# Row units in halves of 512 keys through a ring of three banks, and a down accumulator in the fourth

## The reference

```python
xn = layernorm(x)
q, k, v = (bitnet_linear(xn, w, s) for w, s in ((wq, sq), (wk, sk), (wv, sv)))
scores = einsum('bhqd,bhkd->bhqk', q, repeat(k, 4)) / 4
out = einsum('bhqk,bhkd->bhqd', softmax(scores), repeat(v, 4))
attn = bitnet_linear(out, wo, so)
ffn = (silu(xn @ gate.T) * (xn @ up.T)) @ down.T
return x + attn + ffn
```

## Time and profile before

| what | value |
| --- | --- |
| three timed runs, median (lowest to highest) | 507.28 us (506.56 to 508.65) |
| profiled execution | 506.6 us |
| its span, first to last instruction | 504.9 us |
| granted clock of PE, mean of the span | 0.996 |
| DVE busy in the span | 417.0 us |
| ACT busy in the span | 351.2 us |

### The profile page before, as it was taken

How to read it: one execution, slowest core, us unless ns; L and a number is a source line. 1 busy time by engine, 2 the same in 40 slices (tenths; PEclk the granted TensorE clock), 3 DMA queues, 4 the chain that set the end, 5 groups by cost and what they waited for, 6 DMA issues and landing times.

```text
span 504.9 us, 10418 instructions
## 1 busy us (share of the span) xinstructions
PE 482.1 (95%) x4218; PEld 163.1 (32%) x4218; DVE 417.0 (83%) x487; ACT 351.2 (70%) x655; POOL 93.6 (19%) x138
## 2 busy tenths in 40 slices
PE   1899999999999999999999999999999999999996
PEld 1564444433332222222222222222222223333442
DVE  7879869676778999999999999999999962223985
ACT  1943643352338999999999999999999987874000
POOL 4212245434323000000000000000000103142021
PEclk9999999999998999999999999999999999999999
DMA  8853763732004602102111111120220104463321
GB/s 267 270 94 95 172 142 42 196 76 32 13 0 66 123 23 63 40 24 64 40 32 54 41 49 37 42 61 23 49 55 24 49 28 111 111 152 101 106 79 46
DMA packets 31302, 39.02 MB, mean 77 GB/s; under 512 B 6608, under 2 KB 20816, under 8 KB 31256
## 3 DMA queue, kind: packets, MB, share of 16 engines
q1 hardware_dynamic: 22232, 27.34, 18.8%
q0 software_dynamic: 8304, 10.95, 11.6%
q10 hardware_dynamic: 720, 0.08, 0.1%
HBM read 33.24 MB, written 10.35 MB: 86 GB/s over the span
## 4 chain that ended last, share of the span: by engine, by line
PE 79%; ACT 8%; DVE 6%; DMA 4%; issue 2%; SPq 0%; ACTq 0%; DVEq 0%
PE ps L1257 23%; PE ps L1109 19%; PE ps L1221 13%; PE ps L1118 9%; ACT room L688 6%; PE ps L1183 5%; PE ps L1088 3%; PE ps L1288 3%; DVE nmx L821 3%; PE ps L1170 2%; DMA rsum<-o_scratch 2%; ACT osb L699 1%; DMA hlo<-x 1%; DMA ga<-r_scratch 1%; DVE stats L747 1%
## 5 line engine op out<-in xcount | busy, mean ns | idle before, releaser
L821 DVE TENSOR_REDUCE nmx<-ps 128x1 f32<-128x1024 f32 x256 | 293.8, 1217 | 15.6 <-PE ps L1118 15.4
L688 ACT ACTIVATE room<-ps 128x512 f32<-128x512 f32 x512 | 272.6, 598 | 19.9 <-PE ps L1221 10.0
L1257 PE MATMUL ps<-room,vcur 128*32 128x256 f32 (+1 forms) x1912 | 160.5, 407 | 4.5 <-ACT osb L699 4.1
L1221 PE MATMUL ps<-qst,kB 50*128 50x512 f16 x512 | 148.2, 384 | 1.2 <-DVE room L920 0.5
L1118 PE MATMUL ps<-kA,qst 48*128 48x512 f16 x512 | 145.9, 384 | 0.0
L1109 PE MATMUL ps<-room,wf 128*128 128x512 f16 x448 | 100.6, 379 | 0.0
L1257 PEld LDWEIGHTS ps<-room,vcur 128*32 128x32 f32 x1912 | 37.7, 108 | 103.5 <-issue 56.9
L1221 PEld LDWEIGHTS ps<-qst,kB 50*128 50x128 f16 x512 | 29.8, 93 | 100.2 <-ACT room L688 88.1
L669 ACT ACTIVATE room<-ps,gsc 128x512 f32<-128x512 f32 x28 | 19.2, 686 | 61.0 <-PE ps L1109 61.0
L1109 PEld LDWEIGHTS ps<-room,wf 128*128 128x128 f16 x448 | 42.4, 98 | 55.1 <-issue 7.2
L527 POOL TENSOR_TENSOR hlo<-room,hhi 128x512 f16<-128x512 f32 x28 | 34.0, 1216 | 87.7 <-ACT hhi L599 87.7
(11 more groups left out here) (131 smaller groups left out, 290.5 us busy)
## 6 DMA issues: line engine op xcount, KB each, us to landing
qst<-q_scratch SPq DMA_DIRECT2D x32, 192.0 KB, 3.6
o_scratch<-osb SPq DMA_DIRECT2D x16, 256.0 KB, 2.2
q_scratch<-parts SPq DMA_DIRECT2D x12, 256.0 KB
hlo<-x SPq DMA_DIRECT2D x8, 256.0 KB, 4.9
parts<-x POOLq DMA_DIRECT2D x8, 256.0 KB, 3.4
wf<-gate POOLq DMA_DIRECT2D x14, 128.0 KB, 3.7
wf<-up POOLq DMA_DIRECT2D x14, 128.0 KB, 5.7
wd<-down POOLq DMA_DIRECT2D x1, 1792.0 KB, 13.7
```

The source lines that it names most:

```text
L688: nc.scalar.activation(probs[:, s % 2, r, :], ps[:, bank_of(gp, s, i), :], ACT.Exp, scale=gam_reg[par][r]).then_inc(scores_free, 1)
L821: nc.vector.tensor_reduce(nmx[:, hf, idx:idx + 1], bank_pair(idx % 2), AX.X, ALU.max, negate=True).then_inc(rows_free, 1)
L1221: nc.tensor.matmul(ps[:, bank_of(gp, s, i), :], kB[low:low + SROWS, par, kt % (TT // 2) * P:(kt % (TT // 2) + 1) * P], qst[low:low + SROWS ...
L1257: mm = nc.tensor.matmul(ps[32 * r:32 * r + 32, 7, of], vcur[:, par, key_tile(r, j), :], probs[:, s % 2, r, of], start=(j == 0 and part == ...
```

## The change

Row units of the loop are now computed and reduced tile by tile. Tile n (128 queries by 512 keys) goes into bank n mod 3; PE waits for the reduce of tile n - 3, DVE reduces each tile on its own into `nmx_halves`, and at the end of a half one more reduce joins the two columns of each unit into `nmx` (`max_joined`). The front part's units of the first group stay as they were.

Bank 3 becomes an accumulator of the down projection. From step 10 on, most loop steps end with one fill: 28 fills each for tiles 0, 1 and 2 (steps 10 to 37, 40 to 67, 70 to 97), 12 for tile 3 (steps 100 to 111), 96 in all. The late steps have the other 16 of tile 3, then tile 4 in bank 1 and tile 5 in bank 2: 72 fills, six to four in a step, where there were 112. The tail computes tiles 6 and 7 only. `D_OUT` now gives `down_out` by step of the whole loop, ahead of that step's reduces.

In the late steps the fourth score bank is 0 instead of 3, and the output projection's banks follow.

```diff
@@ -91,12 +91,13 @@
     NU = len(NORM)
 
     O_INVERT, O_NORM, O_SPLIT = [15, 19, 23, 27], [18, 22, 26, 29], [19, 23, 27, 30]
-    FILL = 4
+    FILL = 6
     FILLS = [(i, f, part) for i in range(FILL) for f in range(FT) for part in range(2)]
-    D_OUT = [20, 24, 28]
-
-
-    tail = "O0 C0 O1 O2 C1 C2 O3 D4 D5 O4 O5 D6 O6 O7 D7"
+    LOOP_D = [range(10, 38), range(40, 68), range(70, 98), range(100, 112)]
+    D_OUT = {38: 0, 68: 1, 98: 2, 115: 3, 121: 4}
+
+
+    tail = "O0 C0 O1 O2 C1 C2 O3 D6 O4 O5 O6 O7 D7"
     assert tail.split()[-2:] == [f"O{TT - 1}", f"D{TT - 1}"]
     tail = [(step[0], int(step[1:])) for step in tail.split()]
 
@@ -121,11 +122,22 @@
     assert (BLOCK + 1) % 3 == 0
 
 
-    LATE_SCORES = [4, 5, 6, 3]
-    LATE_T = 2
-    FILL_BANKS = [0, 1]
-    O_BANK = [2, 3, 0, 1]
+    ROW_RING = 3
+    LATE_SCORES = [4, 5, 6, 0]
+    LATE_T = 1
+    FILL_BANKS = [3, 3, 3, 3, 1, 2]
+    O_BANK = [0, 3, 1, 2]
     LATE = (NG - 1) * STEPS
+    QUOTAS = [6, 5, 5] + [5, 5, 5, 5, 4, 4] + [4] * 7
+    assert len(QUOTAS) == STEPS and sum(QUOTAS) + sum(len(r) for r in LOOP_D) == len(FILLS)
+
+    def fills_of(step):
+
+        if step >= LATE:
+            done = len(FILLS) - sum(QUOTAS[step - LATE:])
+            return FILLS[done:done + QUOTAS[step - LATE]]
+        done = sum(1 for r in LOOP_D for n in r if n < step)
+        return FILLS[done:done + 1] if any(step in r for r in LOOP_D) else []
 
     def bank_of(gp, s, i):
 
@@ -454,7 +470,9 @@
                     sp.wait_ge(scores_ready, (v + 1) * REP * TT)
                     load_queries(g + 2, par, hf)
                     if hf == 0:
-                        sp.wait_ge(rows_ready, (g + 1) * 2 * UNITS)
+                        sp.wait_ge(rows_ready, 2 * UNITS)
+                        if g >= 1:
+                            sp.wait_ge(tiles_ready, g * 4 * UNITS)
                         load_keys(kA, kA_loaded, g + 2, par)
                     else:
                         load_keys(kB, kB_loaded, g + 2, par)
@@ -934,14 +952,24 @@
                 elif kind == "A":
                     row_max(n, n // UNITS, n % UNITS)
 
-            def step_rows(gp, s, last):
+            def step_rows(gp, s):
 
                 gp_, par, hf, j = at(gp, s)
-                with_rows = not (last and (par == 1 or s == 2 * STEPS))
-                ga_ = gp_ * 2 + par + 1
-                if with_rows:
-                    row_max(ga_ * (2 * UNITS) + hf * UNITS + 2 * j, hf, 2 * j)
-                    row_max(ga_ * (2 * UNITS) + hf * UNITS + 2 * j + 1, hf, 2 * j + 1)
+                step = gp * (2 * STEPS) + s
+                if step in D_OUT:
+                    down_out(D_OUT[step])
+                if step >= LATE:
+                    return
+                for u in range(2):
+                    for k in range(2):
+                        tile = step * 4 + 2 * u + k
+                        dve.wait_ge(tiles_ready, tile + 1)
+                        nc.vector.tensor_reduce(nmx_halves[:, hf, 2 * j + u, k:k + 1], ps[:, tile % ROW_RING, :], AX.X,
+                                                ALU.max).then_inc(tiles_free, 1)
+                if j == TT - 1:
+                    dve.wait_ge(tiles_free, (step + 1) * 4)
+                    nc.vector.tensor_reduce(nmx[:, hf, :], nmx_halves[:, hf, :, :], AX.X, ALU.max,
+                                            negate=True).then_inc(max_joined, 1)
 
             def invert(u):
 
@@ -968,7 +996,7 @@
                     dve.wait_ge(down_strips_ready, 4 * (i + 1))
                 else:
                     dve.wait_ge(down_ready, i - FILL + 1)
-                bank = FILL_BANKS[i % 2] if i < FILL else i
+                bank = FILL_BANKS[i] if i < FILL else i
                 nc.vector.tensor_tensor(ffn[i], ps[:, bank, :], dsb[:, :], ALU.mult).then_inc(ff_ready, 1)
 
             def rows_out(i):
@@ -976,7 +1004,7 @@
                 dve.wait_ge(oproj_ready, i + 1)
                 if i >= 2:
                     dve.wait_ge(out_ready, i - 1)
-                nc.vector.tensor_tensor(att[:, i % 2, :], ps[:, O_BANK[i % FILL], :], sob[:, :], ALU.mult).then_inc(att_ready, 1)
+                nc.vector.tensor_tensor(att[:, i % 2, :], ps[:, O_BANK[i % len(O_BANK)], :], sob[:, :], ALU.mult).then_inc(att_ready, 1)
                 dve.wait_ge(att_ready, 2 * i + 1)
                 guard(att[:, i % 2, :], H).then_inc(att_ready, 1)
                 if i < TT - 1:
@@ -988,20 +1016,18 @@
                 dve.wait_ge(ff_ready, i + 1)
                 nc.vector.tensor_tensor(ffn[i], ffn[i], att[:, i % 2, :], ALU.add).then_inc(out_ready, 1)
 
-            step_rows(0, 0, False)
+            step_rows(0, 0)
             for gp in range(NP - 1):
                 for s in range(1, 2 * STEPS + 1):
-                    step_rows(gp, s, False)
+                    step_rows(gp, s)
             for s in range(1, 2 * STEPS):
-                step_rows(NP - 1, s, True)
+                step_rows(NP - 1, s)
                 if s in O_INVERT:
                     invert(O_INVERT.index(s))
                 if s in O_NORM:
                     normalize_output(O_NORM.index(s))
                 if s in O_SPLIT:
                     o_low(O_SPLIT.index(s))
-                if s in D_OUT:
-                    down_out(D_OUT.index(s))
 
             down_out(FILL - 1)
             for kind, i in tail:
@@ -1124,8 +1150,21 @@
                 half_rows(par, hf, idx, 0)
                 half_rows(par, hf, idx, 1).then_inc(rows_ready, 1)
 
+            def row_tile(n, par, hf, idx, b):
+
+                head, qt = idx // (HALF // P), idx % (HALF // P)
+                low = b * HI
+                if n < ROW_RING:
+                    pe.wait_ge(rows_free, 2 + 2 * UNITS)
+                else:
+                    pe.wait_ge(tiles_free, n - ROW_RING + 1)
+                nc.tensor.matmul(ps[:, n % ROW_RING, :], qst[low:low + KROWS, par, hf, head, qt * P:(qt + 1) * P],
+                                 kA[low:low + KROWS, par, :], start=True, stop=True).then_inc(tiles_ready, 1)
+
             def transpose_max(v, hf, bank):
-                pe.wait_ge(rows_free, 2 + (v + 1) * UNITS)
+                pe.wait_ge(rows_free, 2 + min(v + 1, 2) * UNITS)
+                if v >= 2:
+                    pe.wait_ge(max_joined, v - 1)
                 nc.tensor.transpose(ps[0:UNITS, bank, 0:P], nmx[:, hf, :], ident[:, :]).then_inc(maxT_ready, 1)
 
             for kind, n in pe_order:
@@ -1162,12 +1201,15 @@
                 if f == 0 and part == 0:
                     if i == 0:
                         pe.wait_ge(wd_loaded, 16)
-                        pe.wait_ge(rows_free, 2 + NG * 2 * UNITS)
-                    elif i >= 2:
-                        pe.wait_ge(ff_ready, i - 1)
+                        pe.wait_ge(rows_free, 2 + 2 * UNITS)
+                    elif FILL_BANKS[i] == 3:
+                        pe.wait_ge(ff_ready, i)
+                    else:
+                        pe.wait_ge(tiles_free, 4 * LATE)
+                        pe.wait_ge(max_taken, 2 * NG)
                 for c in range(P // 32):
                     lo = i * P + c * 32
-                    mm = nc.tensor.matmul(ps[32 * c:32 * c + 32, FILL_BANKS[i % 2], :], (hhi, hlo)[part][:, f, lo:lo + 32],
+                    mm = nc.tensor.matmul(ps[32 * c:32 * c + 32, FILL_BANKS[i], :], (hhi, hlo)[part][:, f, lo:lo + 32],
                                           wd[:, f, :], start=(f == 0 and part == 0),
                                           stop=(f == FT - 1 and part == 1))
                     if f == FT - 1 and part == 1:
@@ -1200,8 +1242,6 @@
                     pe.wait_ge(q_loaded[1 - par][hf], 32 * (gp_ + par + 1))
                     if hf == 0:
                         pe.wait_ge(kA_loaded[1 - par], 32 * (gp_ + par + 1))
-                if not with_rows:
-                    fill = list(range(len(FILLS) * (s - STEPS) // STEPS, len(FILLS) * (s - STEPS + 1) // STEPS))
                 transposes = not (last and s >= STEPS + TT)
                 for i, r in enumerate(ROUND):
                     kt = key_tile(r, j)
@@ -1209,8 +1249,8 @@
                     low = half * HI
                     e = entry(j, i)
                     if step >= LATE:
-                        if LATE_SCORES[i] == 3:
-                            pe.wait_ge(rows_free, 2 + NG * 2 * UNITS)
+                        if LATE_SCORES[i] == 0 and step == LATE:
+                            pe.wait_ge(tiles_free, 4 * LATE)
                         pe.wait_ge(scores_free, 3 + (step - 1) * REP + min(i + 1 + (step == LATE), REP))
                     else:
                         pe.wait_ge(scores_free, block_ * BLOCK + exps_before(e) + 3)
@@ -1221,21 +1261,16 @@
                     nc.tensor.matmul(ps[:, bank_of(gp, s, i), :],
                                      kB[low:low + SROWS, par, kt % (TT // 2) * P:(kt % (TT // 2) + 1) * P],
```

(29 more changed lines are left out.)

## The result

The changed kernel takes 525.45 us (median of four runs, 522.36 to 525.76) against 506.92 us for the kernel before (505.97 to 508.65): 1.0348 times as long, interval 1.0299 to 1.0397. The profiled execution took 525.76 us, its span 524.04.

A forecast was written before the change was run, and what follows sets the result against it. PE was taken as full in the loop with DVE level, and a DMA chain as bounding the late steps. 20.8 + 2.7 - 2.4 + 1.8 + 0.6 - 5.5 = +18.0 on 506.6 gave 524.6, stated as 525; range 515 to 536.

The forecast's parts named there:

- A: Loop: PE sets the pace and each fill is paid in full; total 525, 524 to 530; chance 0.55.
- B: Loop: DVE sets the pace and fills hide in PE's 0.41 us loader gaps; +12.4, total 519; chance 0.2.
- D: Loop: ACT's exps set the pace and nothing added reaches them; loop unchanged, total 502; chance 0.1.
- the join: End of each loop half, DVE: a small extra reduce, 0.2 us, 14 times; 0 if covered, 3 us if not.
- E: Loop fills: strips run one after another, 3 x 0.217 us more per fill; +62, total 587; chance 0.02.
- the three down outputs: Loop steps 38, 68 and 98, on DVE: 0.6 us each, +1.8 us.
- The reduce of 512: Loop, DVE: each 128x512 reduce follows the last in 0.594 us (0.566 to 0.72), making 2.376 us per step.
- C: Loop: the three-bank ring starves DVE; one exposed reduce per step +8, 533; two +22, 547; chance 0.13.
- The loop's sum: Loop: fills +20.8, 16 steps without a fill +2.7, wait for ACT's copy -2.4, down outputs +1.8 us; 22.9 in all.
- The copy's wait: Loop, once per half: values' 0.32 us wait for ACT's bank 7 copy shrinks 0.2 in 12 halves, -2.4 us.
- The late chain: Late steps: 46 us reciprocal-store-broadcast-normalize chain sets their length; a down output adds 0.6, 40 fewer fills (8.7 us) gain 0.
- The tail: After the late steps: two down tiles leave, DVE's 3.50 us passes run without waits, last add earlier; -5.5 us.

## Why the prediction held, point by point

**PE is full, and each fill is paid: right.** The likeliest rival, A, is the one that happened. In the loop a fill costs 1.32 - 1.11 = 0.21 us against the 0.217 of the earlier trace rows, a filled step 2.43 against 2.43, a half 19.85 against some 19.9. The loader's 0.41 us before scores is not room: the strips alone, with no change on DVE, lengthen the old loop by as much. So B (519) and D (502) fall, and the join is covered as forecast. E falls too: the four strips of a fill share a row of 0.40 us. One of the two measures that the Trainium skill's "Perfetto Trace Analysis", Identifying the Most-Contended Engine, has for TensorE, weight loads as a share of time, gives 83.84 of 277.90 us, 30%, for an engine that the runs show to be full; on this loop it misleads.

**The cost is a maximum, and not a sum: the picture was right, and stronger than I had put it.** Against before, without the first half, the strips alone add 19.1 us to the loop, half reduces alone 12.6, both together 20.1. The engines stood level before; each cost on its own slowed the kernel, and the second one came almost free behind the first: the 1.0 between 20.1 and 19.1 is about what the three down outputs cost (below).

**The reduce of 512: right.** Forecast 0.594 us from one to the next, measured 0.598, with 0.683 for one. The errata rule of the Trainium skill's "VectorE: DVE Perf Modes" (section on the TRN2 errata, the table's figure for PSUM sources) gave an estimated 2.63 us of DVE per step; the step that DVE paces takes 2.39, so that here the measurement decides against the rule's figure, though not against its direction: the kernel with half reduces alone is 2.5% slower. C falls: PE waits 0.5 us in all for reduces at row tiles, and the ring's DVE is as fast as that of paired banks.

**The loop's sum was 3.3 us too high** (22.9 forecast, 19.6 measured), through terms that were mis-sized. In the first half, 1.9: its eight steps without a fill should have cost 1.3 more, and it took 0.5 less, 18.80 for 19.34. Part of that is no term of the change: the profile of before had 3.4 us of half clock there, and the same 3.4 us cost the changed kernel's second run 1.2 (20.00 against 18.80). The other 0.7 is that these first steps came cheaper than DVE's pace: with half reduces alone, and no fall of the clock, the first half also took less than a later one, 18.72 for 19.35. The three down outputs took about 1.1 in all instead of 1.8: their halves took 20.03, 20.21 and 19.96 and the half behind the first of them 20.09, 0.89 over the typical one together, though two steps of each of the three have no fill and are 0.04 shorter. The copy's wait gave back more than 2.4: over the steps around it a change of halves cost 0.63 us before and 0.39 after, 0.24 in each of 12 or 13 halves.

**The late chain: right in mechanism, +1.2 for +0.6, and the size within what executions differ by.** The DVE timeline after, to hold against the earlier trace rows:

```profile
431.29 0.54 DVE L978 RECIPROCAL rsum<-rsum 128x64 f32<-128x64 f32 x1
441.05 1.23 DVE L984 TENSOR_TENSOR y<-y,ga 128x1024 f32<-128x1024 f32 x1 [9.22 <-DMA ga<-r_scratch]
442.20 0.68 DVE L1000 TENSOR_TENSOR room<-ps,dsb 128x512 f32<-128x512 f32 x1
442.80 0.54 DVE L978 RECIPROCAL rsum<-rsum 128x64 f32<-128x64 f32 x1
...
478.88 0.69 DVE L984 TENSOR_TENSOR y<-y,ga 128x512 f32<-128x512 f32 x1 [5.83 <-DMA ga<-r_scratch]
```

From the first reciprocal to the fourth normalize 478.88 - 431.29 = 47.6 us, against 46.1 before and 46 to 47 forecast; the down output stands in front of the second reciprocal. In the second run of the same program the late steps took 49.0 and the same stretch of the chain 45.5, less than before the change (in DVE's timeline the waits for the broadcast were 8.92, 10.02, 7.38 and 5.30 us, against 9.22, 10.71, 7.96 and 5.83 here). So the term holds DMA time, which differs by more from one execution to the next than the 0.6 that was forecast; the down output's own share can't be read from these runs. That the 40 fills were worth nothing is shown from both sides: put back they cost nothing, and without the broadcast the stretch is 8 us shorter.

**The tail: the step that failed, -1.7 for -5.5.** The prediction let DVE's passes run from the same distance behind the last exps as before. It did not ask what PE does in the idle time that the removed fills leave. The last wait of ACT's cast and the timelines of PE and of DVE after:

```profile
479.60 0.62 ACT L723 CAST room<-y 128x512 f16<-128x512 f32 x1 [2.87 <-DVE y L984]
...
458.19 2.06 PE L1261 MATMUL ps<-qst,kB 50*128 50x512 f16 x4 [2.95 <-ACT room L706]
460.18 1.93 PE L1292 MATMUL ps<-room,vcur 128*32 128x512 f32 x8
...
482.23 1.94 PE L1292 MATMUL ps<-room,vcur 128*32 128x512 f32 x8 [3.19 <-ACT room L706]
484.10 9.18 PE L1321 MATMUL ps<-sgno,room 128*128 128x512 f16 x32
...
487.73 0.69 DVE L1007 TENSOR_TENSOR room<-ps,sob 128x512 f32<-128x512 f32 x1 [6.19 <-PE ps L1321]
```

And DVE's first pass over an output before:

```profile
464.29 0.69 DVE L979 TENSOR_TENSOR room<-ps,sob 128x512 f32<-128x512 f32 x1 [2.34 <-PE ps L1288]
```

Twice PE stood still for about 3 us, waiting for exps that stand behind the cast and so behind the broadcast, and from the end of each wait (0.5 and 0.6 us before PE starts again) the clock was at 0.50 for 6.8 us. The second of these slows the last values and the first products of the output: 32 matmuls in 9.18 us, for which the second run at full clock shows 7.08. DVE's first pass over an output, at 487.73, starts 5.55 us behind the end of the last exp (482.18) instead of the 2.99 before (461.30). That is 2.6 of the missing 3.8 us, and the second run, which lacks this fall of the clock, has the tail 2.6 shorter. The end of the tail, on DVE and POOL, answers to the earlier trace rows:

```profile
504.50 0.68 DVE L1007 TENSOR_TENSOR room<-ps,sob 128x512 f32<-128x512 f32 x1
505.21 1.00 DVE L828 TENSOR_SCALAR gr<-room 128x512 f32<-128x512 f32 x1
...
508.56 0.68 DVE L1007 TENSOR_TENSOR room<-ps,sob 128x512 f32<-128x512 f32 x1
...
519.75 0.69 DVE L1017 TENSOR_TENSOR wf<-wf,room 128x512 f32<-128x512 f32 x1 [0.80 <-POOL room L511]
...
504.66 1.26 POOL L511 TENSOR_TENSOR wf<-wf,parts 128x512 f32<-128x512 f32 x1 [21.77 <-DVE wf L1000]
```

From the fourth on DVE's passes do run without a wait, as forecast, but one takes 4.06 us instead of 3.50: its first guard step takes 1.00 us beside a POOL addition, where the others take 0.43. From the last add to the end of the span it is 524.04 - 519.75 = 4.29 us against 3.52 before. Here the path that the prediction followed was not the last to end. POOL's closing instruction, a DRAIN, starts beside POOL's last addition and takes the same time in both kernels (from the views of its line before and after: shortest, median and longest length in ns, first and last start in us):

```profile
L146 POOLq DRAIN  x1: 5390/5390/5390, 499.2 to 499.2; - x1
...
L158 POOLq DRAIN  x1: 5385/5385/5385, 518.4 to 518.4; - x1
```

Before, it ended level with SP's DRAIN behind the last store (504.6 and 504.7); after, SP's ended at 522.7 and POOL's at 523.8. So the end followed POOL's last addition, which the prediction itself moved by only 4.7 us (499.21 to 494.5), and not the last add with its 5.5. That is read from the order of the last instructions; no run tests it. The three parts, 2.56, 0.56 and 0.77, add up to 3.9 us for the 3.8 that the tail's term lacks.

So it is luck that 525 came out within half a microsecond: two terms are off in opposite directions, the loop 3.3 below its forecast, late steps and tail 4.4 above. The clock has a part in it too. Three of the four timed runs took 525.18 to 525.76 with a mean granted clock of 0.982 to 0.985, the fourth 522.36 with 0.992; the later run of the same program, whose clock fell for less in the late steps, took 521.68. No version here beats the kernel before. Of those that compute all of the layer, the nearest to it have half reduces with none of the moves (1.0248) or 40 of the fills put back (1.0267, 1.0227 to 1.0307); the interval of the second just touches that of the change.

## What to carry to other kernels

Before moving work into a loop, price the loop's full engines one by one from steps in which the pieces stand alone; a loader's idle time in front of a matmul is no room if the array is still at work, and costs on two level engines count by their maximum. Work removed from a stretch that a DMA chain sets buys nothing there, and the idle time that it leaves on PE can lower PE's clock for the work behind it, as it did in some executions here. When a tail is summed up, follow every engine to its last instruction, and not only the last result.

## What the runs showed of the hardware

- Around the end of stand-stills of PE of 2.95 and 3.19 us the granted clock fell to half, for 6.8 us each time. It did not follow every time: in another execution of the same program the second wait, 2.77 us, had no fall behind it, and the first, 2.25 us, one of 3.4 us. In the ring without loop fills a wait of 1.80 us had a fall of 6.8 us behind it and one of 3.45 us a fall of 3.4 us, so the longer wait did not have the longer fall. With PE kept at work through these waits, none of three executions showed a fall there.
- At the loop's start the clock fell for 0, 3.4 or 10.2 us, and in the third case the first half took 3.8 us more (22.6 against 18.8). It differed between executions of one program.
- A DVE operation of 128x512 (the first step of the guard) took 1.00 us instead of 0.43 while POOL added tiles of the same size. The Trainium skill's "GPSIMD Engine Reference", Key points, says that the two engines share interfaces to the on-chip memory and contend there with some DVE instructions; the traces agree: in each of the eleven profiles the one guard step that lies beside a POOL addition took 0.91 to 1.00 us, and the other seven 0.43. DVE's operations of 128x512 that read PSUM kept their 0.67 to 0.69 us beside the tail's additions.
- POOL's closing DRAIN took 5.38 to 5.39 us in ten profiles and 4.90 in the one without the broadcast, from beside POOL's last addition on.
